# The decay differences and the D product of a Mamba-2 block on GpSimd: one wide instruction, or one for each head

## What is computed

```python
xn = layernorm(x)                                   # (4, 512, 512)
z, xBC, dt = split(xn @ w_in)                       # dt: 16 heads
dt = softplus(dt + dt_bias)
xBC = silu(causal_conv4(xBC));  xh, B, C = split(xBC)
A = -exp(A_log)
# scan in chunks: cs = cumsum(dt * A) inside a chunk
L = exp(cs[l] - cs[s]) for l >= s, else 0           # the decay matrix, one for each head
Y = (C B^T * L) @ (xh * dt) + exp(cs) * (C @ state) # state: decayed and added to, chunk by chunk
Y = Y + xh * D                                      # the D product
y = rmsnorm(Y * silu(z)) * norm_w;  mamba = y @ w_out
h = fwht(silu(xn @ W1.T) * (xn @ W3.T));  ffn = h @ W2.T
out = x + (xn + mamba) + ffn
```

## Time and profile before

| | |
|---|---|
| median of 3 runs | 1006.52 us (1001.41 to 1006.76) |
| profiled execution, its own time | 1008.38 us |
| span in the profile, first to last instruction | 1006.6 us |
| TensorE busy | 941.3 us (94%) |
| VectorE busy | 619.2 us (62%) |
| ScalarE busy | 352.7 us (35%) |
| GpSimd busy | 296.1 us (29%) |
| mean granted TensorE clock | 0.982 |

### The profile page before, as it was taken

One profiled execution on the slowest core, in us unless ns is written; L12 is line 12 of the kernel. 1 busy time (PEld: TensorE's weight loads), 2 busy tenths in 40 slices (PEclk: granted clock), 3 DMA queues, 4 the chain that ended last, 5 costly groups with the idle time before them and its releaser, 6 DMA issues.

```text
span 1006.6 us, 13195 instructions
## 1 busy us (share of the span) xinstructions
PE 941.3 (94%) x4960; PEld 469.3 (47%) x4960; DVE 619.2 (62%) x1063; ACT 352.7 (35%) x537; POOL 296.1 (29%) x180
## 2 busy tenths in 40 slices
PE   3798868999899999999999999999999999999997
PEld 2343333455344444555545445554545445555543
DVE  5776477879543566757862566767751766766621
ACT  5574744443423343331221334332221343232200
POOL 0332241536000111555500202654500202755300
PEclk9899897999899999999999999999999999999999
DMA  9589553746332434553432434554422534355123
GB/s 326 215 303 335 168 178 107 228 129 231 113 117 92 160 96 111 181 137 99 130 84 64 160 95 125 158 147 117 123 63 64 171 96 148 82 157 145 45 74 94
DMA packets 80815, 142.64 MB, mean 142 GB/s; under 512 B 8048, under 2 KB 20976, under 8 KB 78704
## 3 DMA queue, kind: packets, MB, share of 16 engines
q1 hardware_dynamic: 61536, 113.79, 36.5%
q10 hardware_dynamic: 19216, 28.01, 9.6%
HBM read 115.82 MB, written 25.95 MB: 141 GB/s over the span
## 4 chain that ended last, share of the span: by engine, by line
PE 75%; DVE 11%; issue 4%; ACT 4%; DMA 3%; POOL 2%; ACTq 0%; SPq 0%; DVEq 0%; POOLq 0%
PE ps L554 48%; PE ps L759 16%; DVE arena L1147 2%; PE ps L724 2%; DVE arena L1098 2%; DMA arena<-cs_rows 2%; PE ps L716 2%; PE ps L710 1%; PE ps L679 1%; PE ps L696 1%; POOL arena L1340 1%; DVE arena L1168 1%; DVE arena L1129 1%; DMA w_mid<-arena 1%; ACT arena L820 1%
## 5 line engine op out<-in xcount | busy, mean ns | idle before, releaser
L554 PE MATMUL ps<-xh,arena 128*128 128x512 f16 x1600 | 500.7, 386 | 35.5 <-DVE arena L1163 8.8
L554 PE MATMUL ps<-xl,arena 128*128 128x512 f16 x800 | 308.6, 386 | 0.0
L554 PEld LDWEIGHTS ps<-xh,arena 128*128 128x128 f16 x1600 | 160.8, 101 | 233.3 <-issue 34.2
L759 PE MATMUL ps<-arena 128*128 128x512 f16 x768 | 171.2, 379 | 0.0
L1313 POOL TENSOR_TENSOR arena<-arena 128x512 f16<-128x512 f32 x64 | 82.8, 1297 | 280.6 <-ACT arena L899 280.6
L1328 POOL TENSOR_TENSOR arena<-arena 128x2048 f32<-128x2048 f32 x16 | 57.8, 3612 | 291.6 <-DMA arena<-cs_rows 291.6
L1147 DVE SCALAR_TENSOR_TENSOR arena<-ps,cw,arena 128x511 f32<-128x511 f32 (+2 forms) x120 | 89.6, 749 | 52.5 <-ACT arena L889 50.7
L554 PEld LDWEIGHTS ps<-xl,arena 128*128 128x128 f16 x800 | 79.3, 99 | 90.8 <-issue 7.7
L759 PEld LDWEIGHTS ps<-arena 128*128 128x128 f16 x768 | 74.5, 98 | 91.2 <-issue 5.7
L899 ACT ACTIVATE arena<-arena 128x512 f16<-128x512 f32 x64 | 40.3, 630 | 211.0 <-DVE arena L1168 211.0
L554 PE MATMUL ps<-wo_hi,arena 128*128 128x512 f16 x256 | 78.8, 379 | 0.6 <-DVE arena L1276 0.6
(11 more groups left out here) (158 smaller groups left out, 1074.2 us busy)
## 6 DMA issues: line engine op xcount, KB each, us to landing
arena<-w_parts SPq DMA_DIRECT2D x198, 256.0 KB, 2.7
w_parts<-arena SPq DMA_DIRECT2D x66, 256.0 KB, 3.4
arena<-cs_rows ACTq DMA_DIRECT2D x16, 1024.0 KB, 6.1
arena<-w SPq DMA_DIRECT2D x8, 1024.0 KB, 8.5
arena<-w SPq DMA_DIRECT2D x32, 256.0 KB, 4.0
arena<-ecs_rows ACTq DMA_DIRECT2D x24, 256.0 KB, 7.7
arena<-w SPq DMA_DIRECT2D x8, 512.0 KB, 6.0
w_mid<-arena SPq DMA_DIRECT2D x16, 256.0 KB, 2.2
```

Of the source, the lines that this page charges most:

```text
L554: ins = nc.tensor.matmul(out_ap, lhs(i, a), rhs(i, c), start=(i == 0 and s == 0), stop=(i == n - 1 and s == 2))
L759: ins = nc.tensor.matmul(bank(t), hw[a][:, i, t * P:(t + 1) * P], w2s[i % W2R][:, d, :], start=(i == 0 and s == 0), stop=(i == JF - 1 and ...
```

## The change

In step `E` the two wide instructions on GpSimd and the one-column instruction between them are replaced by sixteen tensor_scalar instructions of 128 columns, one for each head. Each reads its part of `csbc`, subtracts the head's value of `cs_s` as a scalar for each partition, and takes the minimum with 0 in the same pass. `emin_ok` is signalled by the last; `esub_ok` is gone and its two waiters now wait for `emin_ok`. The lower clamp is no longer made there: instead VectorE clamps dt * A at -1e35 with one more instruction of 64 columns, once for a batch, behind L1065. The D product in step `T` becomes eight tensor_scalar instructions of 128 columns with the value of D as a scalar for each partition.

```diff
-        esub_ok = signal("esub_ok", NC, 1)
-        emin_ok = signal("emin_ok", NC)
+        emin_ok = signal("emin_ok", NC, 1)
...
                     elif kind == "HL":
-                        sp.wait_ge(esub_ok.sem, esub_ok.at(0, NC - 1))
+                        sp.wait_ge(emin_ok.sem, emin_ok.at(0, NC - 1))
...
                         act.wait_ge(d_cst, (b + 1) * 32)
-                        act.wait_ge(esub_ok.sem, esub_ok.at(b, c - 1))
+                        act.wait_ge(emin_ok.sem, emin_ok.at(b, c - 1))
...
-            nc.vector.tensor_tensor(heads(av), heads(dtv), nega[:].unsqueeze(1).to_broadcast([P, NC, NH]),
-                                    ALU.mult).then_inc(dt_a.sem, 1)
+            k = steps.step(nc.vector.tensor_tensor(heads(av), heads(dtv), nega[:].unsqueeze(1).to_broadcast([P, NC, NH]), ALU.mult))
+            dve.wait_ge(steps.sem, k)
+            nc.vector.tensor_scalar(av, av, -1.0e35, None, ALU.max).then_inc(dt_a.sem, 1)
...
-                        nc.gpsimd.tensor_tensor(Eb, csbc, cs_s[:, c * NH:(c + 1) * NH].unsqueeze(2).to_broadcast([P, NH, P]),
-                                                ALU.subtract).then_inc(esub_ok.sem, 1)
-                        pool.wait_ge(esub_ok.sem, esub_ok.at(b, c))
-                        nc.gpsimd.tensor_tensor(pool_mark[:], ones[:, 0:1], ones[:, 0:1], ALU.mult)
-                        nc.gpsimd.tensor_scalar(Eb, Eb, 0.0, -3.0e38, ALU.min, ALU.max).then_inc(emin_ok.sem, 1)
+                        for h in range(NH):
+                            ins = nc.gpsimd.tensor_scalar(Eb[:, h, :], csbc[:, h, :], cs_s[:, c * NH + h:c * NH + h + 1], 0.0,
+                                                          ALU.subtract, ALU.min)
+                        ins.then_inc(emin_ok.sem, 1)
...
-                        nc.gpsimd.tensor_tensor(XD.rearrange("p (q l) -> p q l", q=QE), XT[:, 0:QE, c * P:(c + 1) * P],
-                                                dcol[:].unsqueeze(2).to_broadcast([P, QE, P]), ALU.mult).then_inc(xd_ok.sem, 1)
+                        for q in range(QE):
+                            ins = nc.gpsimd.tensor_scalar(XD[:, q * P:(q + 1) * P], XT[:, q, c * P:(c + 1) * P], dcol[:, q:q + 1],
+                                                          None, ALU.mult)
+                        ins.then_inc(xd_ok.sem, 1)
```

More of the change, by code:

```diff
@@ L215, in build @@
         nws = sb("nws", [P, QE])
-        pool_mark, first = sb("pool_mark", [P, 1]), sb("first", [P, 1])
+        first = sb("first", [P, 1])
         f_in, f_half0, f_half, f_13, f_out, f_w2, f_had = (
```

## The result

The changed kernel takes 1059.62 us in the median of 4 runs (1050.43 to 1062.59), against 1004.93 (1001.41 to 1006.76) for the kernel before in the same comparison: ratio 1.0533, 95% interval 1.0457 to 1.061. It is slower by 5%, where 1% faster was forecast, and it lies far outside the range. The profiled execution took 1062.13, its span is 1060.3 us; that is 53.7 over the span before.

The account below looks back on a forecast made before the run. TensorE bounds the kernel, waiting for VectorE, which GpSimd instructions keep off a shared port. Gains of 4.8 (chunk 0, batches 1 to 3), 1.0 (chunk 2) and 4.8 (batch 0) make 10.6: 996 us, range 991 to 1007.

Parts of the forecast that it names:

- What bounds it, the port: VectorE instructions with two SBUF inputs wait for a port each GpSimd instruction holds; it changes hands between queued GpSimd instructions.
- the three waits of 1.6: TensorE's waits for late L1147 at E of chunk 0, batches 1 to 3; all go, winning 4.8 us.
- Rival A: The sixteen E instructions act as one port hold, so VectorE loses E's whole length; 1013.7 us, chance 0.14.
- C: Rival: VectorE is on time, but TensorE next waits for ScalarE or GpSimd; half the gain goes, 1001.2 us, chance 0.12.
- The price of one instruction: Each new 128-column GpSimd instruction in E and D costs 0.27 us, between 0.21 and 0.43.
- E, "GpSimd gains 1.3": In each E step 5.6 us on GpSimd are replaced by 4.3, a gain of 1.3 us.
- D, forecast at 0.3 longer: D product: 1.90 us on GpSimd replaced by 2.2, while its port hold falls from 1.9 to 0.27.
- Chunk 2, "Xdec starts 1.0 earlier": Chunk 2, batches 1 and 2: E 1.3 shorter, D 0.3 longer, so Xdec starts 1.0 earlier; 1.0 us won.
- rival B: Each instruction costs 0.43 with the port shared; chunk 2 loses 9.6 us, so no change, 1007.3 us, chance 0.14.
- Batch 0, 4.8: Four places in batch 0 where VectorE loses time to E or D: 5.1 us won, less 0.3 for the clamp.
- The moved waits: The next chunk's csbc DMA and SP's HL step wait for E's end, 0.7 us later, hidden by several tiles.
- VectorE's clamp: The extra 64-column clamp, 0.23 us four times, costs nothing in batches 1 to 3 and 0.3 us in batch 0.

Follow-up runs that it names:

- e13: The changed kernel with min and max with constants in all sixteen E and eight D instructions (results not computed); ratio 0.9861, median 991.92 us.
- e5: The changed kernel with one full-width instruction in place of the sixteen and one in place of the eight (wrong scalars); 1010.87 us against 1007.46.
- e11: The changed kernel with Xdec ahead of the eight D instructions; ratio 1.002 to the kernel before.
- e7: The kernel before with E's subtraction and clamp each cut into four instructions of 512 columns; ratio 0.9929, median 1000.25 us.
- e3: The kernel before with E's clamp (min and max with constants) cut into sixteen instructions of 128 columns; 1017.36 us against 1007.23.
- e12: The kernel before with eight instruction forms in 128-column pieces, four in place of the clamp, four in place of D; 1052.27 us against 1006.77.
- e9: The changed kernel with constants in place of the scalars from memory in E and D; ratio 1.0247 to the kernel before.
- e6: The changed kernel with a second operation, maximum with a constant, in each of the eight D instructions; 1070.65 us.
- e4: The kernel before with E's subtraction as sixteen tensor_tensor instructions of 128 columns, the clamp left as one; 1012.33 us against 1007.23.
- e2: The kernel before with only the D product cut into eight instructions; ratio 1.0133, median 1021.14 us against 1007.23.

## Why the prediction was wrong

- *What bounds it, the port:* right. L1129 went from 3.69 to 0.86 us at the longest, VectorE is busy for 41 us less, the three waits of 1.6 are gone, and in e13, where E had the price of the forecast and D 0.36 us an instruction, 14 us were won against the 10.6 of the sum. Rival A (one hold) fell: VectorE gets in between sixteen instructions queued without a wait. So did C: no wait with another name stands in the place of the three.
- *The price of one instruction:* the step that failed. The forecast took 0.27 us for each, with a high end of 0.43; measured are 0.69 in E and 0.58 in D, from start to start. The fixed part (0.1 to 0.19, and up to 0.13 for the scalar) was near enough: 0.26 measured. The term that was mis-sized is the columns, 0.11 us in the forecast against 0.43 and 0.32. They were taken at 0.86 ns from L1332, which is a pair of min and max with constants, as if the number of inputs were all that mattered; the form of the change takes 3.4 and 2.5 ns. There was no row of this form, and the one row that I used was of other operations, so the bound for a column should have been left open upward.
- *E, "GpSimd gains 1.3":* wrong by that price; it loses 5.5. Merging two passes into one saved nothing, since the one pass is slower than both (7.16 us in e5 against 5.6). D, forecast at 0.3 longer, is 2.7 longer (8 x 0.58 against 1.90), without VectorE's instructions in between.
- *Chunk 2, "Xdec starts 1.0 earlier":* counted from the start of E it starts 10.7 later. This is the mechanism of rival B, with a price over its bound. B's own working gives, with 0.69 and 0.58, 5.5 more for E, 2.7 for D and 2 for L1234, 10.2 in a place; measured waits are 6.3, 10.8 and 10.3 us in batches 1 to 3. That two of them come so near is in part luck, since the waits also follow the csbc DMA, which took 4.8, 9.3 and 8.8 us there. B looked at chunk 2 of two batches only. Of the 52.3 us, 25 are elsewhere: 3.35 at chunk 1 and 2.11 at chunk 0 in each of three batches, 2.7 and 5.9 in batch 0. And it left out the half clock at the long waits, 14 us.
- *Batch 0, 4.8:* in e13 TensorE's waits of over 0.5 us between 130 and 275 us add up to 11.3 us, against 17.5 before; 6.2 less, where 5.1 was forecast ahead of the clamp. In the change itself the longest of them, for L1204, grew from 5.0 to 7.4.
- *The moved waits, VectorE's clamp:* nothing in TensorE's waits names them, and in the chain at chunk 2 of batches 1 to 3 the csbc DMA starts right behind ScalarE's L898, not at the end of an E.
- *The other side of the sum:* the prediction let GpSimd's 71% of free time cover everything but chunk 2 of two batches. It did, as e11 shows, outside the stretch from the csbc DMA to Xdec; the slack of that stretch should have been listed for every chunk, since two lengthenings of it share it.

## What to carry to other kernels

An instruction form that the kernel has never used on an engine has no known price, not even with the same width and number of inputs; time it alone before counting on it, at two widths, so that the price of a column and the fixed part come apart. Splitting a GpSimd instruction gave VectorE its port back, and four pieces were enough for it here (e7); what is split has to be off the chain, or be put behind what TensorE waits for. When two steps of one chain get longer, add them before asking whether the slack covers them: 10 and 13 us alone were 54 together.

## What the runs showed of the hardware

GpSimd tensor_scalar, 128 partitions, 128 columns fp32, from start to start: 0.26 us with min and max with the constants 0 and -3e38 (e3, e12), but 0.36 with 1e30 and -3e38 (e13); 0.49 with min alone and 0.50 with multiply alone (e12), 0.60 with the two other pairs tried, min and add, subtract and min (e9, e12). A scalar from memory adds 0.08 (e9 against the change), a second operation 0.11 (e6). The forms with a scalar take 2.5 ns a column with one and 3.4 with two operations (e5), against 0.86 for min and max. A tensor_tensor with one broadcast input takes 0.36 for 128 columns (e4, e12) and 1.0 for 512 (e7); for 128 columns it multiplies by a column of scalars in 0.36, where tensor_scalar takes 0.58. In the changed kernel TensorE's granted clock was at 0.50 at the eight waits for Xdec of 2.7 us and more, and its four matmuls right behind them took 3.4 to 3.8 us; at the three of 2.1 they took 1.96, at a clock of 1.00. This is no rule for the length of a wait: in e2, behind waits of 2.1, they took 1.96 once and 3.6 twice.
